# A fused layer-norm, expert and state-space kernel: softplus in one table set, diagonal states spread out, tiles of B taken from SBUF

## The chip, the cores and the metric

The kernel runs on one core of a Trainium2 chip. The metric is device time in microseconds (us) of one execution. The engines are PE (TensorE, matmul), DVE (VectorE), ACT (ScalarE), POOL (GpSimd) and SP (SyncE, which issues the plain DMAs). Each engine runs its own instructions in order and waits for the others by semaphores.

## The reference, cut to what matters

Four sequences of 512 tokens with 256 channels go through three parts: half an expert feed-forward, a selective state-space layer with 16 states, half the same feed-forward again. The change touches the middle part only:

```python
x_proj = x @ W_x.T
dt_x, Bm, Cm = jnp.split(x_proj, [R, R + N], axis=-1)      # R = 64, N = 16
dt = jax.nn.softplus(dt_x @ W_dt.T + b_dt)
dA = jnp.exp(jnp.einsum('bld,dn->bldn', dt, -jnp.exp(A_log)))
dBx = jnp.einsum('bld,bln,bld->bldn', dt, Bm, x)
h = dA_t * h + dBx_t                                        # scan over l
y_t = jnp.einsum('bdn,bn->bd', h, C_t)                      # plus x * D
```

## The kernel before, in words

A batch is one sequence. Channels lie on the partitions in two halves k = 0, 1, so one state of one batch is a tile of 128 x 1024 (two halves of 512 time steps). There are 64 states in all, s = 16 b + n, and each goes through a fixed line of engines:

- ACT: `decay(s)` writes da, two Exp of 128x511 (L663).
- dBx is made in one of two ways. In a *plain* state, dt x (tile `dtx_t`, time on the partitions) is multiplied by one column of B for each of four blocks of 128 time steps; ACT makes some of the four tiles (`outer`, L679, B read from `b_t` in SBUF) and DVE the others (`outer`, L1405, B read from `B_T`, which lies in the PSUM bank `Y`). `BY_DVE` says how many tiles DVE makes. PE then transposes the four tiles into a PSUM bank pair (`turn_dbx`, L1030). In a *diagonal* state (`DIAG`), PE multiplies `dtx_t` by a 256 KB block-diagonal matrix of B (L1037), which SP has loaded from memory (L384) into one of two buffers; no tile is made.
- DVE: the scan h = da h + dBx (L1421), da in SBUF and dBx in PSUM.
- POOL: the product gs = h C (L523), both operands in SBUF, C loaded by SP (L354).
- PE: `add(s)` transposes the product into the sum `YA` in PSUM (L1054). It also frees one of the two gs buffers for POOL.

The rings: four da and hs buffers (the scan of s waits for the product of s-4), two gs buffers (the product of s waits for `add(s-2)`), three plain tiles.

While batch b is scanned, batch b+1 is prepared: `project` (PE, L983), `project_copy` (ACT, L630), `project_bt` (PE transposes B into `B_T`, L994; DVE copies it into `b_t`, L1361), `project_z` (PE, L1003), softplus, `turn_dt` (PE, L1014) and `project_dtx` (DVE, L1390). Softplus is written as max(z,0) + ln(1+e) plus a rounding correction, with e = exp(-|z|). ACT does Abs, Relu (L637), Exp (L641), Identity (L650) and Ln (L657, a table set of its own); DVE does L1370 (for batch 0 the two lines L1373 and L1375), L1381 and L1384, each with one operand in a PSUM bank. All batches after the first use the one bank `T`, one half at a time.

At the turn from one batch to the next, DVE's `add_y` (L1457) adds `YA` to x after the last `add` of the batch, between the scans of n = 1 and n = 2, and takes the statistics of the result (L1177) after n = 2. POOL normalises tiles of 128x256 (L469) after the products of n = 5 to 8 (6 to 9 in batch 0) and eight such tiles before batch 0.

Before batch 0 there is a prologue: softplus(0), the last shared-expert gate `shared_gate(0, 3, 1)` (Tanh, L576), `turn_dt(0)`, the first tiles. In batch 3, ACT also does four Tanh pieces (L584).

Of the kernel before, what the change touches and what calls it, by code (L numbers as in the profile page):

```python
# [27 lines left out]
def macaron_kernel(nc, x, w_xT, w_dtT, b_dt, a_log, d_skip, router_w, gate_w, up_w, down_w,  # L28
# [23 lines left out]
    BY_DVE = ((2, 2, 2, 1, 1, 1) + (0,) * 6 + (1, 0, 1, 0),) + ((1, 1, 0, 1) + (0,) * 6 + (1, 0, 1, 0, 1, 0),) * 2 + ((0,) * 16,)  # L52
    DIAG = (tuple(range(6, 12)),) + (tuple(range(4, 10)),) * 2 + ((4, 7, 9, 13),)
# [6 lines left out]
    SHARED = E  # L60
    assert D == F == KC * P and L == 512 and GT == 16 and E == 8 and NR == 18 and N == 16
# [14 lines left out]
    with ExitStack() as ctx:  # L76
# [3 lines left out]
        def sem(name):  # L80
# [22 lines left out]
        neg_half = sb("neg_half", [P, LT])  # L103
        e_less = sb("e_less", [P, E])
# [123 lines left out]
        pj_all, pj_copy, pj_bt, pj_btc, pj_z, pj_abs, pj_max, pj_exp, pj_u, pj_w, pj_rest, pj_ln, pj_sum, pj_dt, pj_tp, pj_dtx = (  # L228
            sem(f"pj_{s}") for s in ("all", "copy", "bt", "btc", "z", "abs", "max", "exp", "u", "w", "rest", "ln", "sum", "dt", "tp",
# [191 lines left out]
        def _(pool):  # L421
# [8 lines left out]
            nc.gpsimd.memset(neg_half[:], -0.5)  # L430
            nc.gpsimd.memset(before[:], 1.0)
# [125 lines left out]
        def _(act):  # L557
# [85 lines left out]
            def project_u(b, k):  # L643

                if k == 0:
                    act.wait_ge(pj_exp, b + 1)
                    act.wait_ge(pj_max, KC * (b + 1))
                else:
                    act.wait_ge(pj_dt, KC * b + 1)
                nc.scalar.activation(pj_bank(b, k), w_exp[:, k], ACT.Identity, bias=1.0).then_inc(pj_u, 1)  # L650

            def project_ln(b):

                act.wait_ge(pj_exp, b + 1)
                if b > 0:
                    act.wait_ge(pj_sum, KC * b)
# [93 lines left out]
            nc.scalar.preload_act_table(ACT.Exp)  # L750
# [30 lines left out]
        def _(pe):  # L781
# [4 lines left out]
            def ln_transposes(c, q):  # L786
                pe.wait_ge(ln_xn, GT * c + 2 * q + 2)
                if c == 2:
# [197 lines left out]
            def project_bt(b):  # L986
# [4 lines left out]
                else:  # L991
                    pe.wait_ge(sc_dve, states_by("dve", N * (b - 1) + 4 + 3))
# [12 lines left out]
            def turn_dt(b, h):  # L1005

                pe.wait_ge(pj_dt, KC * (b + 1))
                if b > 0 and h > 0:
                    pe.wait_ge(pj_dtx, 2 * b + h)
                dst = YA[h] if b == 0 else T  # L1010
# [55 lines left out]
            def scan(b):  # L1066
                more = b + 1 < BATCH
                for n in range(N):
                    s = N * b + n
                    if more and n == 3:  # L1070
# [14 lines left out]
                    late = (2, 1, 0, 0)[b]  # L1085
# [4 lines left out]
                    if more and n - int(b == 0) in (8, 10):  # L1090
                        turn_dt(b + 1, (n - 8) // 2)
# [74 lines left out]
        def _(dve):  # L1166
# [384 lines left out]
```

## Time and profile before

| | us |
|---|---|
| median of 3 runs | 441.34 (440.18 to 441.75) |
| the profiled execution | 441.44 |
| its span, first to last instruction | 439.6 |
| first scan to last product of POOL | 142.8 to 330.1 |

Busy shares over the span are PE 92%, DVE 75%, ACT 63%, POOL 64%; the granted TensorE clock is 0.996. A share over the span mixes the expert parts, where PE is busy, with the scan, which takes some 187 us of the 440. A timeline row reads: start, duration of the merged run, engine, line, operation, output and inputs, count, and in brackets the idle time before it and what ended it. The duration of a single instruction overlaps the next one's by some 0.08 us on DVE, so the step from one start to the next is a little shorter.

### The profile page before, as it was taken

To read this page: it belongs to the slowest core of one execution; us is meant where nothing else is said; L and a number is where in the kernel's file an instruction comes from. 1 tells how busy PE (TensorE), PEld (TensorE's weight loads), DVE (VectorE), ACT (ScalarE), POOL (GpSimd) and SP (SyncE) were. 2 spreads that over 40 slices of the span, in tenths; PEclk is the share of its full clock that TensorE was granted. 3 is DMA by queue.
4 is the path that set the end of the run, shared out by engine and by line. 5 is a ranking of instruction groups with operands and counts; after the bars stand their busy time and mean duration, and the time that the engine had idled before them with its cause. 6 is when DMAs were issued, how large, how long until landed. Compare 5 with 4: busy or idle time off the path is not lost. (4 is left out here: it accounts for less than half of the span.)

```text
span 439.6 us, 8329 instructions
## 1 busy us (share of the span) xinstructions
PE 402.4 (92%) x2716; PEld 278.4 (63%) x2716; DVE 329.5 (75%) x518; ACT 275.0 (63%) x501; POOL 281.1 (64%) x216
## 2 busy tenths in 40 slices
PE   6899899999996899899989997989999899899995
PEld 5537444444454689777977797879994556344452
DVE  4678565553388988999999999989887775456552
ACT  1430465564248799897999899997962210556553
POOL 7204356643328589997999799988891006487553
PEclk9899999999999999999999999999999999999999
DMA  8958115842604226463536453443320534334311
GB/s 250 385 179 264 48 54 167 284 174 101 204 10 91 73 82 180 81 144 106 186 75 118 141 176 73 115 157 92 121 72 0 172 107 120 99 118 135 111 60 48
DMA packets 50808, 56.84 MB, mean 129 GB/s; under 512 B 16329, under 2 KB 35597, under 8 KB 50768
## 3 DMA queue, kind: packets, MB, share of 16 engines
q1 hardware_dynamic: 46624, 45.78, 35.0%
q0 software_dynamic: 4144, 10.54, 8.0%
q8 instruction: 23, 0.38, 0.4%
q14 instruction: 17, 0.14, 0.1%
HBM read 41.14 MB, written 16.48 MB: 131 GB/s over the span
## 5 line engine op out<-in xcount | busy, mean ns | idle before, releaser
L523 POOL TENSOR_TENSOR gs<-hs,c_sb 128x1024 f32<-128x1024 f32 x63 | 148.3, 2380 | 18.7 <-DVE hs L1421 11.4
L1421 DVE TENSOR_TENSOR_SCAN hs<-da,bank 128x1024 f32<-128x1024 f32 x64 | 144.1, 2273 | 4.1 <-PE bank L1030 2.1
L663 ACT ACTIVATE da<-dt_sb,a_neg 128x511 f32<-128x511 f32 x128 | 84.5, 713 | 2.4 <-DVE dt_sb L1384 1.2
L1054 PE MATMUL bank<-ident,gs 128*128 128x128 f32 x504 | 66.3, 275 | 7.5 <-POOL gs L523 5.9
L1054 PEld LDWEIGHTS bank<-ident,gs 128*128 128x128 f32 x504 | 55.9, 141 | 12.1 <-POOL gs L523 9.8
L679 ACT ACTIVATE dbx_t<-dtx_t,h_sb 128x256 f32<-128x256 f32 x145 | 62.1, 498 | 1.6 <-DVE dtx_t L1390 1.4
L879 PE MATMUL bank<-xnT,w_gu 128*128 128x512 f32 x112 | 50.8, 601 | 0.0
L1030 PE MATMUL bank<-ident,dbx_t 128*128 128x128 f32 x336 | 44.2, 274 | 6.8 <-DVE hs L1421 4.1
L477 POOL DMA_INDIRECT da<-rows,row_token x29 | 30.6, 1055 | 29.7 <-DVE row_token L1292 21.2
L1030 PEld LDWEIGHTS bank<-ident,dbx_t 128*128 128x128 f32 x336 | 37.5, 141 | 12.2 <-DVE hs L1421 5.9
L591 ACT ACTIVATE th<-bank,da 128x256 f32<-128x256 f32 x36 | 17.0, 473 | 43.1 <-PE bank L918 30.4
L918 PE MATMUL bank<-w_gu,tt 128*128 x72 | 35.6, 616 | 3.2 <-ACT tt L596 2.2
L498 POOL DMA_INDIRECT token_out<-y_sb,row_token x18 | 19.0, 1056 | 29.2 <-DVE y_sb L1338 26.3
L477 POOL DMA_INDIRECT da<-rows,row_half x14 | 14.7, 1054 | 35.5 <-DVE row_token L1297 27.2
L1328 DVE TENSOR_TENSOR h_sb<-th,bank 128x256 f32<-128x256 f32 x36 | 15.1, 420 | 28.0 <-ACT th L591 27.9
L915 PE MATMUL bank<-w_gu,tt 128*32 x72 | 34.3, 598 | 1.4 <-ACT tt L596 1.4
L879 PEld LDWEIGHTS bank<-xnT,w_gu 128*128 128x128 f32 x112 | 21.0, 194 | 22.4 <-issue 22.3
L915 PE MATMUL bank<-dtx_t,tt 128*32 128x512 f32 x72 | 34.3, 598 | 0.0
L574 ACT ACTIVATE hs<-bank 128x512 f32<-128x512 f32 x10 | 6.0, 597 | 40.0 <-PE bank L879 34.6
L596 ACT ACTIVATE tt<-bank 128x512 f32<-128x512 f32 (+1 forms) x40 | 22.1, 553 | 13.6 <-PE bank L933 12.3
L498 POOL DMA_INDIRECT out<-y_sb,row_token x18 | 19.8, 1098 | 16.1 <-DVE y_sb L1341 8.2
L562 ACT ACTIVATE xnT<-bank 128x512 f32<-128x512 f32 x24 | 13.9, 590 | 17.3 <-PE bank L807 17.2
(184 smaller groups left out, 787.1 us busy)
## 6 DMA issues: line engine op xcount, KB each, us to landing
c_sb<-c_dram SPq DMA_DIRECT2D x64, 256.0 KB, 3.3
rows<-xn_no SPq DMA_DIRECT2D x8, 516.0 KB, 5.4
diag_dram<-dbx_t SPq DMA_DIRECT2D x6, 512.0 KB
routing<-diag_dram SPq DMA_DIRECT2D x11, 256.0 KB, 2.8
slot_m<-diag_dram SPq DMA_DIRECT2D x11, 256.0 KB, 2.9
rows<-xn_no SPq DMA_DIRECT2D x1, 2064.0 KB, 9.4
x_sb<-in_x SPq DMA_DIRECT2D x4, 512.0 KB, 6.4
w_gu<-in_gate_w SPq DMA_DIRECT2D x2, 1024.0 KB, 10.2
```

What stands on the lines that cost most here:

```text
L477: nc.gpsimd.indirect_dma_start(out=xr[:, u, lo:hi], out_offset=None, in_=source, in_offset=bass.IndirectOffsetOnAxis(ap=row, axis=0), boun ...
L498: nc.gpsimd.indirect_dma_start(out=rows_back, out_offset=bass.IndirectOffsetOnAxis(ap=row_token[:, TILE[j]:TILE[j] + 1], axis=0), in_=y_sb ...
L523: nc.gpsimd.tensor_tensor(gs[:, s % 2], hs[:, s % RING], c_sb[:, s % RING].unsqueeze(1).to_broadcast([P, KC, L]), ALU.mult).then_inc(sc_g, 1)
L596: nc.scalar.activation(tt[:, (j + 1) % 2, lo:hi], T[:, lo * P:hi * P].rearrange("p (a t) -> p a t", t=P), ACT.Copy).then_inc(ff_tpc, 1)
L663: nc.scalar.activation(da[:, s % RING, k, 1:L], dt_sb[:, k, seq(s // N)][:, 1:L], ACT.Exp, scale=a_neg[:, k, s % N:s % N + 1]).then_inc(sc ...
L679: step = nc.scalar.activation(plain_buffer(s)[:, i, :], dtx_t[:, b % 2, i, :], ACT.Copy, scale=b_t[:, b, i, n:n + 1])
L879: last = nc.tensor.matmul(shared_banks(r, b, fo)[h], w_gu[:, k, SHARED, h * F + fo * P:h * F + (fo + 1) * P], xnT[:, k, b * L:(b + 1) * L] ...
L915: last = nc.tensor.matmul(H[j % 2][part, :], tt[:, j % 2, 2 + k, part], gu_part(i, g)[:, k, :] if g else w, start=(k == 0), stop=(k == KC ...
L918: last = nc.tensor.matmul(H[j % 2][:, :], tt[:, j % 2, 2 + k], w, start=(k == 0), stop=(k == KC - 1))
L1030: mm = nc.tensor.transpose(DBX[s % 2][:, k, i * P:(i + 1) * P], plain_buffer(s)[:, i, k * P:(k + 1) * P], ident[:])
L1054: mm = nc.tensor.matmul(YA[k][:, i * P:(i + 1) * P], products[:, k, i * P:(i + 1) * P], ident[:], start=(s % N == 0 and i == 0), stop=(s % ...
L1421: nc.vector.tensor_tensor_scan(hs[:, s % RING].rearrange(flat), da[:, s % RING].rearrange(flat), DBX[s % 2][:, :, :].rearrange(flat), 0.0, ...
```

## The change

- Softplus is rebuilt. ACT loads the set `natural_log_exp_and_others` by name, twice: before the first layer-norm copies, and again after `shared_gate(0, 3, 1)`. Relu goes; Identity becomes one instruction of 1024 that writes -(1+e) into SBUF (`neg_u`: half of `dtx_t` for batch 0, `y_sb` for the others). DVE then does `project_rest` (one of 1024, both inputs in SBUF), `project_max` (two of 512, one input in PSUM), `project_dt` (one of 1024, both inputs in SBUF) and `project_dtx` (one of 1024; two of 512 for batch 0).
- The two halves of z get a bank each (`T` and `Y`), so `B_T` in `Y` must have been copied away before the second half is written. `project_bt` on PE moves from n = 3 to n = 2, 1, 0 in batches 0, 1, 2, where it stands ahead of `turn_dbx(s+2)` and `add(s-1)`; DVE's copy moves from n = 4 to n = 3, 2, 1.
- DVE's `outer` reads B from `b_t` in SBUF, in all batches.
- In batches 1 and 2 the diagonal states are 4, 6, 8, 10, 12, 14 (before 4 to 9), and DVE makes one tile of each of the states 0 to 3 (before 0, 1, 3, 10, 12, 14).

```diff
-    BY_DVE = ((2, 2, 2, 1, 1, 1) + (0,) * 6 + (1, 0, 1, 0),) + ((1, 1, 0, 1) + (0,) * 6 + (1, 0, 1, 0, 1, 0),) * 2 + ((0,) * 16,)
-    DIAG = (tuple(range(6, 12)),) + (tuple(range(4, 10)),) * 2 + ((4, 7, 9, 13),)
+    BY_DVE = ((2, 2, 2, 1, 1, 1) + (0,) * 6 + (1, 0, 1, 0),) + ((1, 1, 1, 1) + (0,) * 12,) * 2 + ((0,) * 16,)
+    DIAG = (tuple(range(6, 12)),) + (tuple(range(4, 16, 2)),) * 2 + ((4, 7, 9, 13),)
...
+        def neg_u(b):
+            return dtx_t[:, 1].rearrange("p (k a) d -> p k (a d)", k=KC) if b == 0 else sg_h
...
-                nc.scalar.activation(dt_sb[:, k, seq(b)], pj_bank(b, k), ACT.Relu, bias=b_sb[:, k:k + 1]).then_inc(pj_max, 1)
...
-                nc.scalar.activation(pj_bank(b, k), w_exp[:, k], ACT.Identity, bias=1.0).then_inc(pj_u, 1)
+                nc.scalar.activation(neg_u(b), w_exp[:], ACT.Identity, bias=neg_one[:, 0:1], scale=-1.0).then_inc(pj_u, 1)
...
-            nc.scalar.preload_act_table(ACT.Exp)
+            nc.scalar.preload_act_table_set(EXP_LN)
...
             shared_gate(0, 3, 1)
+            nc.scalar.preload_act_table_set(EXP_LN)
...
-                    if more and n == 3:
+                    late = (2, 1, 0, 0)[b]
+                    if more and n == late:
                         project_bt(b + 1)
...
+            def project_rest(b):
+                dve.wait_ge(pj_u, b + 1)
+                nc.vector.scalar_tensor_tensor(out=neg_u(b), in0=neg_u(b), scalar=1.0, in1=w_exp[:],
+                                               op0=ALU.add, op1=ALU.add).then_inc(pj_rest, 1)
+            def project_max(b):
+                dve.wait_ge(pj_rest, b + 1)
+                for k in range(KC):
+                    nc.vector.scalar_tensor_tensor(out=neg_u(b)[:, k], in0=pj_bank(b, k), scalar=b_sb[:, k:k + 1], in1=neg_u(b)[:, k],
+                                                   op0=ALU.add, op1=ALU.max).then_inc(pj_max, 1)
...
-                nc.vector.tensor_tensor(pj_bank(b, k), log_w[:, k], pj_bank(b, k),
-                                        ALU.add if b == 0 else ALU.subtract).then_inc(pj_sum, 1)
-                dve.wait_ge(pj_sum, KC * b + k + 1)
-                nc.vector.tensor_tensor(dt_sb[:, k, seq(b)], pj_bank(b, k), dt_sb[:, k, seq(b)], ALU.add).then_inc(pj_dt, 1)
+                dve.wait_ge(pj_max, KC * (b + 1))
+                nc.vector.tensor_tensor(dt_sb[:, :, seq(b)], log_w, neg_u(b), ALU.add).then_inc(pj_dt, 1)
...
                 nc.vector.tensor_tensor(plain_buffer(s)[:, LT - mine:, :], dtx_t[:, b % 2, LT - mine:, :],
-                                        B_T[:, b, LT - mine:, n:n + 1].to_broadcast([P, mine, D]), ALU.mult).then_inc(sc_dve, 1)
+                                        b_t[:, b, LT - mine:, n:n + 1].to_broadcast([P, mine, D]), ALU.mult).then_inc(sc_dve, 1)
...
-                    if more and n == 4:
+                    if more and n == (3, 2, 1)[b]:
                         project_bt(b + 1)
...
+                    if more and n == 5 + late:
+                        project_rest(b + 1)
+                    if more and n == 6 + late:
+                        project_max(b + 1)
+                    if more and n == 7 + late:
+                        project_dt(b + 1)
+                    if more and n == 11 + late:
+                        project_dtx(b + 1)
```

## Rows read from the trace of the kernel before

**Rows 1.** Busy time by engine, the sum of 140 to 330 us:

```profile
sum 190.00, PE 176.61 PEld 158.46 DVE 179.97 ACT 170.83 POOL 170.45; mean PE 9.30 PEld 8.34 DVE 9.47 ACT 8.99 POOL 8.97
```

**Rows 2.** Timeline of POOL in the scan:

```profile
181.21 14.02 POOL L523 TENSOR_TENSOR gs<-hs,c_sb 128x1024 f32<-128x1024 f32 x6
...
271.84 23.53 POOL L523 TENSOR_TENSOR gs<-hs,c_sb 128x1024 f32<-128x1024 f32 x10
297.62 2.37 POOL L523 TENSOR_TENSOR gs<-hs,c_sb 128x1024 f32<-128x1024 f32 x1 [2.24 <-DVE hs L1421]
```

**Rows 3.** Timeline of DVE at the turn from batch 2 to 3:

```profile
289.39 1.28 DVE L1457 TENSOR_TENSOR x_sb<-x_sb,bank 128x512 f32<-128x512 f32 x2 [1.18 <-PE bank L1054]
290.59 2.28 DVE L1421 TENSOR_TENSOR_SCAN hs<-da,bank 128x1024 f32<-128x1024 f32 x1
```

**Rows 4.** Timeline of ACT in the prologue:

```profile
129.31 0.68 ACT L637 ACTIVATE dt_sb<-bank,b_sb 128x512 f32<-128x512 f32 x1
129.88 0.69 ACT L636 ACTIVATE w_exp<-bank,b_sb 128x512 f32<-128x512 f32 x1
...
131.02 1.07 ACT L641 ACTIVATE w_exp<-w_exp 128x1024 f32<-128x1024 f32 x1
132.11 1.28 ACT L657 ACT_TABLE_LOAD   x1
```

**Rows 5.** Timeline of DVE, last softplus step of the prologue and batch 0:

```profile
136.83 0.69 DVE L1384 TENSOR_TENSOR dt_sb<-bank,dt_sb 128x512 f32<-128x512 f32 x1
...
148.07 0.41 DVE L1405 TENSOR_TENSOR dbx_t<-dtx_t,bank 128x256 f32<-128x256 f32 x1
...
172.38 0.70 DVE L1370 SCALAR_TENSOR_TENSOR bank<-bank,w_exp 128x512 f32<-128x512 f32 x1 [0.74 <-ACT bank L650]
```

**Rows 6.** Timeline of PE, start of batch 0 and the turn to batch 2:

```profile
153.96 1.04 PE L1030 MATMUL bank<-ident,dbx_t 128*128 128x128 f32 x8
...
205.02 0.42 PE L994 MATMUL bank<-ident,th 16*128 16x16 f32 x4
...
208.13 1.95 PE L1037 MATMUL bank<-routing,dtx_t 128*128 128x128 f32 x16
...
240.52 1.88 PE L983 MATMUL bank<-xnT,w_x 128*96 128x512 f32 x4
242.24 1.04 PE L1030 MATMUL bank<-ident,dbx_t 128*128 128x128 f32 x8
243.11 1.04 PE L1054 MATMUL bank<-ident,gs 128*128 128x128 f32 x8
```

**Rows 7.** DMA issues: count, KB each, median us to landing:

```profile
routing<-diag_dram SPq DMA_DIRECT2D x11, 256.0 KB, 2.8
...
diag_dram<-h_sb SPq DMA_DIRECT2D x22, 2.0 KB, 3.7
```

**Rows 8.** Timeline of ACT at the start of batch 0:

```profile
154.16 0.59 ACT L630 ACTIVATE th<-bank 96x512 f32<-96x512 f32 x1 [2.26 <-PE bank L983]
```

**Rows 9.** Timeline of POOL at the start of batch 0:

```profile
145.15 4.87 POOL L523 TENSOR_TENSOR gs<-hs,c_sb 128x1024 f32<-128x1024 f32 x2 [4.12 <-DVE hs L1421]
...
163.29 2.38 POOL L523 TENSOR_TENSOR gs<-hs,c_sb 128x1024 f32<-128x1024 f32 x1 [0.41 <-PE bank L1054]
```

**Rows 10.** Single lines: count, duration min/median/max in ns, first and last start:

```profile
L1450 DVE TENSOR_TENSOR dbx_t<-hs,c_sb x2: 678/968/1259, 329.4 to 330.6; 128x512 f32<-128x512 f32 x2
L1405 DVE TENSOR_TENSOR dbx_t<-dtx_t,bank x20: 393/403/686, 139.7 to 274.1; 128x256 f32<-128x256 f32 x17, 128x512 f32<-128x512 f32 x3
L1357 DVE TENSOR_TENSOR x_sb<-xn_no,x_sb x3: 1217/1224/1225, 116.7 to 126.9; 128x1024 f32<-128x1024 f32 x3
L469 POOL TENSOR_SCALAR xn_no<-x_sb,mv,rstd x20: 1209/1221/1260, 131.4 to 270.7; 128x256 f32<-128x256 f32 x20
```

**Rows 11.** Timeline of all engines at the last product, POOL and DVE:

```profile
327.78 2.35 POOL L523 TENSOR_TENSOR gs<-hs,c_sb 128x1024 f32<-128x1024 f32 x1 [0.52 <-PE bank L1054]
...
329.42 1.86 DVE L1450 TENSOR_TENSOR dbx_t<-hs,c_sb 128x512 f32<-128x512 f32 x2
```

More of the change, by code:

```diff
@@ L227, in macaron_kernel @@
         a_ready = sem("a_ready")
-        pj_all, pj_copy, pj_bt, pj_btc, pj_z, pj_abs, pj_max, pj_exp, pj_u, pj_w, pj_rest, pj_ln, pj_sum, pj_dt, pj_tp, pj_dtx = (
-            sem(f"pj_{s}") for s in ("all", "copy", "bt", "btc", "z", "abs", "max", "exp", "u", "w", "rest", "ln", "sum", "dt", "tp",
+        pj_all, pj_copy, pj_bt, pj_btc, pj_z, pj_abs, pj_max, pj_exp, pj_u, pj_rest, pj_ln, pj_dt, pj_tp, pj_dtx = (
+            sem(f"pj_{s}") for s in ("all", "copy", "bt", "btc", "z", "abs", "max", "exp", "u", "rest", "ln", "dt", "tp",
                                      "dtx"))
@@ L701, in scan @@
                         project_exp(1)
-                        project_u(1, 0)
-                    if b < BATCH - 1 and n == 7 + int(b == 0):
-                        project_u(b + 1, 1)
+                    if b == 0 and n == 5:
+                        project_u(1)
                     if b == 0 and n == 6:
@@ L1005, in turn_dt @@
             def turn_dt(b, h):
[L1007 to L1010, printed above, removed]
+                pe.wait_ge(pj_dt, b + 1)
+                dst = pj_bank(b, h)
                 for i in range(2):
@@ L1089, in scan @@
                         skip(b, n - 5)
-                    if more and n - int(b == 0) in (8, 10):
-                        turn_dt(b + 1, (n - 8) // 2)
+                    if more and n - int(b == 0) in (8, 9):
+                        turn_dt(b + 1, n - int(b == 0) - 8)
                     turn = 12 if more else 9
@@ new lines, in project_dtx @@
+            def project_dtx(b):
+                halves = ((0, 1), (1, 2)) if b == 0 else ((0, 2),)
+                for lo, hi in halves:
+                    dve.wait_ge(pj_tp, 2 * b + hi)
+                    src = pair[3 if b == 0 else 1][:, lo:hi].rearrange("p h (i d) -> p (h i) d", d=D)
+                    nc.vector.tensor_tensor(dtx_t[:, b % 2, 2 * lo:2 * hi], src, xn[:, LT * b + 2 * lo:LT * b + 2 * hi, :],
+                                            ALU.mult).then_inc(pj_dtx, hi - lo)
@@ L1434, in scan @@
                         stats_of(2, b - 1)
[L1435 removed]
+                    late = int(b == 0)
+                    if more and n == (3, 2, 1)[b]:
                         project_bt(b + 1)
[L1437 to L1443 removed]
+                    if more and n == 5 + late:
[6 more added lines that the diff above has]
+                        project_dtx(b + 1)
             def last_product():
@@ L1492, in _ @@
             shared_hidden(0, 3, 0)
-            for k in range(KC):
-                project_w(0, k)
-            for k in range(KC):
-                project_dt(0, k)
-            for h in range(2):
-                project_dtx(0, h)
+            project_rest(0)
+            project_max(0)
+            project_dt(0)
+            project_dtx(0)
             outer(0)
```

63 lines of the change are left out of this document (21 added, 42 removed).

## The prediction

> **What bounds the kernel now.** I read the scan alone, since the change touches nothing else. First the busy time by engine over 140 to 330 us [rows 1]: VectorE is busy for 180 of 190 us, ScalarE for 171, GpSimd for 170. By that view VectorE is the bound, but a mean over four batches says nothing about which wait ends last. So next GpSimd's own timeline [rows 2]: 14.02 us for six products is 2.34 us each, 23.53 us for ten is 2.35, without a gap. The ten that begin at 271.84 are states 9 to 15 of batch 2 and 0 to 2 of batch 3. The reader is to see that inside a batch GpSimd always finds a finished scan. It idles only at a turn: 2.24 us before product 3 of batch 3. VectorE's timeline at that turn says why [rows 3]: product 15 ends at 271.84 + 7 x 2.353 = 288.31, TensorE adds it, `add_y` starts at 289.39 (an idle time ended by that add), the scan of n = 2 follows, then statistics and the scan of n = 3. The chain is thus GpSimd through a batch, then TensorE and VectorE through the turn. Time taken from ScalarE or VectorE in mid-batch buys nothing as long as GpSimd finds its scans ready; time put on GpSimd, or on the path to `add_y`, counts in full.
>
> **Softplus in one set.** In the prologue VectorE and ScalarE are the chain. Two Relus go at a step of 129.88 - 129.31 = 0.57 us [rows 4], so Exp ends 1.14 us earlier, at 130.95. The Identity of 1024 isn't shown; I take the Exp of that shape, 1.06, so it ends near 132.0, and Ln, without its load of 1.28 [rows 4], near 133.1. On VectorE, `project_rest` and `project_dt` have both inputs in SBUF at 1024, as the combine of 1.22 us [rows 10]; the two halves of `project_max` take 0.69 each at most [rows 5], 1.25 with overlap. 132.0 + 1.22 + 1.25 + 1.22 = 135.7 against 136.83 + 0.69 = 137.52 now [rows 5]: 1.8 us earlier, if nothing else stands in the way. On ScalarE the Tanh gate now takes a load before and a named load after it (133.1 + 1.28 + 0.6 + 1.28 = 136.3); that is hidden behind VectorE's `project_dtx` and first tile, and costs 0.6 at most if they come sooner.
>
> In batches 0 to 2, ScalarE loses two loads and two Relus and gains two tiles in batches 1 and 2; VectorE loses about 0.5 us of softplus (eight of some 0.69 against 3 x 1.22 + 2 x 0.69) and two tiles of 0.40 [rows 10]. The wait of 0.74 us at 172.38 [rows 5] may go too. All of that lies beside GpSimd's products: I count 0, with 4.5 us as the other end (1.4 of waits, 1.5 and 1.6 of work; a rival below). One load for the first Tanh of batch 3 is at most 1.28; I take 0, ScalarE being 19 us short of full [rows 1].
>
> **The diagonal states.** As many as before. A pair of a diagonal and a plain state costs TensorE, by steps (0.87 from 242.24 to 243.11 [rows 6], and 1.95 less the same 0.17 of overlap), 1.78 + 0.87 for dBx and 2 x 0.87 for the adds: 4.39 us against GpSimd's 4.69 for two products. So TensorE keeps up: 0, with 0.4 a pair as the bound where a turn of dt or xn falls in the pair. SP still issues six loads and six writes a batch, but loads at n = 9, 11, 13 now stand among the writes for the next batch and ahead of C loads. A load has at least two products, 4.7 us, before TensorE wants it; it lands in 2.8 and a write in 3.7 [rows 7]. I count 0; were they served strictly in turn, 3.7 + 2.8 - 4.7 = 1.8 us a time.
>
> **`project_bt` moved forward.** It waits for ScalarE's `project_copy`, and behind it on TensorE now stand `turn_dbx` and `add`. At the start of batch 0, `turn_dbx` of state 4 ran at 153.96 [rows 6], while the copy starts only at 154.16 and takes 0.59 [rows 8]. With 0.42 for the transposes of B [rows 6], `turn_dbx` starts at 155.17, 1.2 late, and so do `add(1)`, scan 4 and GpSimd's product 3, which needs that add. GpSimd's idle 0.41 at 163.29 [rows 9] swallows a part: 0.8. At the turn from batch 1 to 2, `project(3)` runs from 240.52 to 242.40, and `turn_dbx` and the last add followed at 242.24 and 243.11 [rows 6]. The copy (0.59) and the transposes (0.42) now come between: 243.4, again 1.2 late, all of it on `add_y`. In batch 1 the copy is old: nothing. Sum 2.0, bounds 0.8 and 2.4.
>
> **B from SBUF.** This decides. The one VectorE multiplication in the scan with both inputs in SBUF is the last product, L1450. Its two instructions took 1259 and 678 ns [rows 10]. The first started at 329.42, under a GpSimd product that ran from 327.78 to 330.13 [rows 11]; 329.42 + 1.26 = 330.68, which is GpSimd's end plus 0.55, about the work of 512 columns. The tiles of L1405, one input in PSUM, stayed at 393 to 403 ns (686 for the wide ones) in the same company [rows 10]. So I read: VectorE with two SBUF inputs doesn't run beside a GpSimd instruction that reads SBUF; it waits for its end. One event, but a sharp one. What GpSimd loses while VectorE runs, no row shows: between 0 and VectorE's whole duration. I take the whole, since two that can't run together in one order hardly can in the other.
>
> The Trainium skill says this outright ("SBUF — State Buffer", section "Who interferes with whom"): a VectorE instruction with two SBUF inputs and a GpSimd instruction that reads SBUF share a read interface, and the later one blocks for the whole of the earlier. The trace agrees with VectorE's half (1.26 against 0.68 us); that GpSimd blocks too, no run here shows. By the rule the sum is the one below; by the row alone it is the first rival.
>
> The change makes 4 `project_rest`, 4 `project_dt` and 16 tiles of that kind.
> - Prologue: rest, dt and the tiles of states 0, 1, 2 meet eight back-to-back normalisations of 1.22 us from 131.4 on [rows 10]. Each waits 0 to 1.22; five at the mean of 0.61 are 3.05. With the 1.8 gained: +1.25, bounds -1.8 and +4.3.
> - Start of batch 0: the tile of state 4 comes at 148.07 [rows 5], with products 0 and 1 running from 145.15 to 150.02 [rows 9]. It waits 1.95; scan 2, the last shared result, `add(0)` and `project(1)` are queued behind it: +2.0, bounds 0 and 2.35. Tiles 3 and 5 meet an idle GpSimd.
> - Inside the batches GpSimd stands still for six of 1.22 (rest and dt of batches 1 to 3) and eight tiles of 0.40 (states 12 and 14 of batch 0; 0, 1, 2 of batches 1 and 2): 7.3 + 3.2 = +10.5, bounds 0 and 10.5. States 3 of both batches fall where GpSimd waits anyway. VectorE's own waits, half a product or 1.17 each, fall into its lead over GpSimd: 0; the other end is 1.17 at the six and at four first tiles, +11.7.
>
> Sum: 1.25 + 2.0 + 0.8 + 1.2 + 10.5 = 15.75. The profiled execution took 441.44 us (span 439.6), the median 441.34, so they are one basis: 457 us.
>
> **Rivals.**
> - *Only VectorE waits; GpSimd loses nothing.* For it: the row shows no more. Against: sharing would then be one-sided. 441.4 + 1.25 + 2.0 + 2.0 = 446.7.
> - *VectorE is shut out.* Products follow each other every 2.34 us at 2.35 each [rows 2], so no gap may open until GpSimd runs out of scans. Then each of ten occasions (six large, four first tiles) costs GpSimd the instruction and a scan of 2.28 [rows 3]: 6 x 3.50 + 4 x 2.68 = 31.7, in all 441.4 + 1.25 + 4.0 + 31.7 = 478. Against: L1450 ran as soon as GpSimd ended, though nothing came after it there.
> - *Nothing excludes anything*, and the 1.26 us had another cause: -1.8 + 2.0, 441.6 us, no change.
> - *Faster: VectorE is the bound after all*, and nothing excludes. For it: 180 of 190 us [rows 1]. Against: no gap in GpSimd's runs. It decides if GpSimd finds a scan unfinished in mid-batch. Then 1.8 of the prologue, waits of 1.4 in batch 0, 0.5 a batch of softplus and four tiles of 0.40 come off, less 2.0 for `project_bt`: 441.4 - 1.8 - 1.4 - 1.5 - 1.6 + 2.0 = 437.1.
>
> **How the numbers follow.** The forecast gets 0.58 (its own range 449 to 464, from half of GpSimd's loss to a part of VectorE's waits), one-sided waiting 0.12, shut out 0.07, no change 0.13, faster 0.10. Slower is the first three less what spills, 0.76; same 0.13; faster 0.11. About 0.5%, 2.2 us, is what this kernel's measurement can tell from no change. The range 440 to 467 leaves out the faster case and the shut-out one.
>
> **What would show it.** Right: `project_rest`, `project_dt` and the tiles have long and scattered durations, ending a constant time after a GpSimd product; products beside them exceed 2.38 us or show gaps; GpSimd busy or blocked grows by some 10 us; `turn_dbx` of state 4 and the last add of batch 1 wait for L630; no table load is left in batches 0 to 2. Wrong: those VectorE instructions hold 1.22 and 0.40 us under a running product, or GpSimd's runs break in mid-batch for want of scans.

## The result, and the profile after

The changed kernel takes 458.85 to 463.95 us in three runs, 460.02 in the middle, against 440.81 us (440.18 to 441.75) for the kernel before. A fourth run, at 466.91, is over 1.5% above the fastest, counts as slow and is left out. The ratio is 1.0455, with a 95% interval of 1.0374 to 1.0535: slower by 4.6%, some 20 us. The forecast was 457.0, range 440 to 467.

The profiled execution took 458.85 us, its span 457.1, so 17.5 us more span than before. It is the shortest of the three; where the others lose up to 5 us more, no trace shows. The same instruction in both traces says where they came in: this is by how much later it starts after the change.

| from | to | later at the end by | gained in between |
|---|---|---|---|
| start of the kernel | first scan | 0.2 | 0.2 |
| first scan | add of state 0 | 2.0 | 1.8 |
| add of state 0 | POOL product 3 of batch 0 | 4.75 | 2.75 |
| there | POOL product 3 of batch 1 | 7.3 | 2.55 |
| there | POOL product 0 of batch 2 | 12.85 | 5.55 |
| there | POOL product 1 of batch 2 | 14.85 | 2.0 |
| there | POOL product 3 of batch 3 | 17.5 | 2.65 |

Nothing is lost behind that: the last product is 17.5 late too. POOL's timeline in the scan, whose rows of before are in [rows 2, 9]:

```profile
131.51 11.69 POOL L476 TENSOR_SCALAR xn_no<-x_sb,mv,rstd 128x256 f32<-128x256 f32 x8
145.34 4.87 POOL L530 TENSOR_TENSOR gs<-hs,c_sb 128x1024 f32<-128x1024 f32 x2 [2.15 <-DVE hs L1425]
154.59 2.34 POOL L530 TENSOR_TENSOR gs<-hs,c_sb 128x1024 f32<-128x1024 f32 x1 [4.38 <-PE bank L1059]
160.79 2.36 POOL L530 TENSOR_TENSOR gs<-hs,c_sb 128x1024 f32<-128x1024 f32 x1 [3.86 <-PE bank L1059]
...
178.12 2.19 POOL L476 TENSOR_SCALAR xn_no<-x_sb,mv,rstd 128x256 f32<-128x256 f32 x1
...
187.52 14.57 POOL L530 TENSOR_TENSOR gs<-hs,c_sb 128x1024 f32<-128x1024 f32 x6
...
216.07 5.68 POOL L530 TENSOR_TENSOR gs<-hs,c_sb 128x1024 f32<-128x1024 f32 x2
221.73 1.22 POOL L476 TENSOR_SCALAR xn_no<-x_sb,mv,rstd 128x256 f32<-128x256 f32 x1
...
225.26 2.21 POOL L476 TENSOR_SCALAR xn_no<-x_sb,mv,rstd 128x256 f32<-128x256 f32 x1
...
234.50 11.70 POOL L530 TENSOR_TENSOR gs<-hs,c_sb 128x1024 f32<-128x1024 f32 x5
248.75 4.98 POOL L530 TENSOR_TENSOR gs<-hs,c_sb 128x1024 f32<-128x1024 f32 x2 [2.56 <-DVE hs L1425]
...
259.17 2.37 POOL L530 TENSOR_TENSOR gs<-hs,c_sb 128x1024 f32<-128x1024 f32 x1 [2.37 <-PE bank L1059]
```

Two kinds of loss stand in it. First, instructions that became longer. A normalisation (L476) of 1.22 us takes 2.19 and 2.21; two products take 5.68 where an undisturbed pair takes 4.70; six take 14.57 against 14.02 in [rows 2]. Second, gaps: 4.38 and 3.86 at the start of batch 0, and in batch 1 one of 2.56 for want of a scan, in mid-batch, where before there was none. The two gaps at the start of batch 0 in the kernel before, 1.81 and 2.75 us shorter:

```profile
152.58 2.35 POOL L523 TENSOR_TENSOR gs<-hs,c_sb 128x1024 f32<-128x1024 f32 x1 [2.57 <-PE bank L1054]
156.04 2.36 POOL L523 TENSOR_TENSOR gs<-hs,c_sb 128x1024 f32<-128x1024 f32 x1 [1.11 <-PE bank L1054]
```

DVE's timeline names what stood against them:

```profile
148.27 2.21 DVE L1409 TENSOR_TENSOR dbx_t<-dtx_t,h_sb 128x256 f32<-128x256 f32 x1
...
176.71 2.51 DVE L1385 TENSOR_TENSOR dt_sb<-tt,y_sb 128x1024 f32<-128x1024 f32 x1
...
193.04 1.80 DVE L1409 TENSOR_TENSOR dbx_t<-dtx_t,h_sb 128x256 f32<-128x256 f32 x1
...
218.06 1.47 DVE L1371 SCALAR_TENSOR_TENSOR y_sb<-y_sb,w_exp 128x1024 f32<-128x1024 f32 x1 [1.46 <-ACT y_sb L658]
...
225.14 1.23 DVE L1385 TENSOR_TENSOR dt_sb<-tt,y_sb 128x1024 f32<-128x1024 f32 x1
...
241.15 5.33 DVE L1409 TENSOR_TENSOR dbx_t<-dtx_t,h_sb 128x256 f32<-128x256 f32 x1
```

Line these up with POOL's rows. The tile at 148.27 ends at 150.48, and POOL's pair of products at 145.34 + 4.87 = 150.21. The tile at 241.15 ends at 246.48, and POOL's run of five at 234.50 + 11.70 = 246.20. Both end 0.27 to 0.28 us after POOL, one after 2.21 us and one after 5.33; undisturbed, a tile takes 0.40. That is VectorE waiting for GpSimd. The row at 225.14 shows the other direction: `project_dt` starts first and takes an undisturbed 1.23, until 226.37; POOL's normalisation, started at 225.26, is the one that takes 2.21, 0.99 more. So between a VectorE instruction and a product, whichever comes second waits, and so does a normalisation that comes second. A normalisation that is already under way is another matter. POOL and DVE in the prologue:

```profile
134.98 1.22 POOL L476 TENSOR_SCALAR xn_no<-x_sb,mv,rstd 128x256 f32<-128x256 f32 x1
...
135.52 1.23 DVE L1385 TENSOR_TENSOR dt_sb<-tt,dtx_t 128x1024 f32<-128x1024 f32 x1
```

`project_dt` starts 0.54 us into that normalisation, and both take their undisturbed time. In e4, e5 and e7, below, the same instruction does so too (1.23 us each).

The third loss is on PE, in its timeline at the start of batch 0 and at the turn from batch 1 to 2, where before has [rows 6]:

```profile
153.32 1.09 PE L1059 MATMUL bank<-ident,gs 128*128 128x128 f32 x8 [3.68 <-DVE x_sb L1308]
154.25 3.37 PE L990 MATMUL bank<-xnT,w_x 128*96 128x512 f32 x4
158.30 0.42 PE L1001 MATMUL bank<-ident,th 16*128 16x16 f32 x4 [0.68 <-ACT th L637]
...
248.73 1.09 PE L1035 MATMUL bank<-ident,dbx_t 128*128 128x128 f32 x8 [3.08 <-DVE hs L1425]
...
251.24 1.97 PE L1035 MATMUL bank<-ident,dbx_t 128*128 128x128 f32 x8
...
256.68 0.42 PE L1001 MATMUL bank<-ident,th 16*128 16x16 f32 x4 [0.68 <-ACT th L637]
```

and the two stretches by themselves (the last columns are the granted clock, the DMA share and GB/s):

```profile
150.00:160.00 10.00, 6.00 (x28) 3.34 (x29) 6.24 (x7) 4.16 (x10) 2.55 (x2) 0.83 0.21 66
250.00:260.00 10.00, 9.24 (x50) 6.51 (x48) 7.18 (x7) 5.57 (x12) 6.79 (x4) 0.83 0.38 125
```

`project` takes 3.37 us where it took 1.88, and eight transposes take 1.97 instead of 1.09. In both stretches PE had just stood still, for 3.68 and 3.08 us, behind a late VectorE, and the granted clock is 0.83. With two levels, 2.4 and 1.2 GHz, 0.83 over 10 us means 3.4 us at the lower one.

### The profile page after: what moved, and what is told of

It reads as the page before. It is cut to its first block and busy times, and to the rows that moved or that the text cites. A ratio compares the mean times of both kernels' runs of the same rounds, so it can differ in the third digit from the quotient of the medians.

```text
span 457.1 us, 8294 instructions
## 1 busy us (share of the span) xinstructions
PE 406.7 (89%) x2716; PEld 279.2 (61%) x2716; DVE 340.2 (74%) x501; ACT 267.8 (59%) x490; POOL 289.3 (63%) x217
## 5 line engine op out<-in xcount | busy, mean ns | idle before, releaser
L530 POOL TENSOR_TENSOR gs<-hs,c_sb 128x1024 f32<-128x1024 f32 x63 | 150.7, 2412 | 27.5 <-PE bank L1059 14.3
L1059 PEld LDWEIGHTS bank<-ident,gs 128*128 128x128 f32 x504 | 57.0, 142 | 11.8 <-POOL gs L530 7.9
L687 ACT ACTIVATE dbx_t<-dtx_t,h_sb 128x256 f32<-128x256 f32 x149 | 63.6, 496 | 0.8 <-DVE dtx_t L1393 0.8
L1035 PE MATMUL bank<-ident,dbx_t 128*128 128x128 f32 x336 | 45.3, 279 | 11.0 <-DVE hs L1425 7.6
L886 PE MATMUL bank<-xnT,w_gu 128*128 128x512 f32 x112 | 51.9, 612 | 0.0
L476 POOL TENSOR_SCALAR xn_no<-x_sb,mv,rstd 128x256 f32<-128x256 f32 x20 | 29.5, 1479 | 0.0
```

Source lines behind the costliest of these rows:

```text
L476: nc.gpsimd.tensor_scalar(xn[:, i], x_sb[:, i, :], mv[:, i, 0:1], rstd[:, i:i + 1], ALU.subtract, ALU.mult).then_inc(ln_xn, 1)
L530: nc.gpsimd.tensor_tensor(gs[:, s % 2], hs[:, s % RING], c_sb[:, s % RING].unsqueeze(1).to_broadcast([P, KC, L]), ALU.mult).then_inc(sc_g, 1)
L687: step = nc.scalar.activation(plain_buffer(s)[:, i, :], dtx_t[:, b % 2, i, :], ACT.Copy, scale=b_t[:, b, i, n:n + 1])
L886: last = nc.tensor.matmul(shared_banks(r, b, fo)[h], w_gu[:, k, SHARED, h * F + fo * P:h * F + (fo + 1) * P], xnT[:, k, b * L:(b + 1) * L] ...
L1035: mm = nc.tensor.transpose(DBX[s % 2][:, k, i * P:(i + 1) * P], plain_buffer(s)[:, i, k * P:(k + 1) * P], ident[:])
L1059: mm = nc.tensor.matmul(YA[k][:, i * P:(i + 1) * P], products[:, k, i * P:(i + 1) * P], ident[:], start=(s % N == 0 and i == 0), stop=(s % ...
```

## Experiments

Each is a variant of one of the two kernels. Ratios are to the kernel before, run on the same chip.

**B from SBUF alone** (e1): before, and only VectorE's tiles read B from SBUF.

```diff
+                    dve.wait_ge(pj_btc, b + 1)
...
-                                        B_T[:, b, LT - mine:, n:n + 1].to_broadcast([P, mine, D]), ALU.mult).then_inc(sc_dve, 1)
+                                        b_t[:, b, LT - mine:, n:n + 1].to_broadcast([P, mine, D]), ALU.mult).then_inc(sc_dve, 1)
```

> The kernel before, with one thing changed: VectorE's tiles read B from SBUF instead of PSUM. Theory (VectorE with two SBUF inputs and GpSimd exclude each other, and GpSimd is the path): the tile of state 4 in batch 0 waits 2 us for a product, some 13 tiles inside the batches stop GpSimd for 0.4 us each, and one or two tiles may be shut out for more than one product as the tile of 5.33 us in the changed kernel was; 448 to 453 us. Rival (the tiles are cheap, and softplus or the moved transposes made the loss): within 1.5 us of 441.

Measured: 453.36 us, ratio 1.029 (1.0261 to 1.0319). One operand moved from PSUM to SBUF costs 12 us. DVE's timeline, then POOL's at the same place:

```profile
181.42 4.61 DVE L1406 TENSOR_TENSOR dbx_t<-dtx_t,h_sb 128x256 f32<-128x256 f32 x1
...
193.62 1.03 DVE L1406 TENSOR_TENSOR dbx_t<-dtx_t,h_sb 128x256 f32<-128x256 f32 x1
```

```profile
181.05 4.70 POOL L523 TENSOR_TENSOR gs<-hs,c_sb 128x1024 f32<-128x1024 f32 x2
188.31 2.37 POOL L523 TENSOR_TENSOR gs<-hs,c_sb 128x1024 f32<-128x1024 f32 x1 [2.56 <-DVE hs L1422]
```

The tile comes under the first of two products, lets a boundary between them pass, and ends at 186.03, 0.28 us after the second. By then VectorE is a scan behind, and GpSimd waits 2.56 us for it. The shut-out of the changed kernel thus occurs without its other parts. The six runs spread from 449.29 to 456.85 us, the profiled one being the shortest, and those of the kernel before from 440.44 to 442.71. That runs differ in which tiles are shut out would explain it, but no trace shows it.

**The schedule alone** (e2): before, with the new `DIAG` and `BY_DVE` of batches 1 and 2, B still read from PSUM.

```diff
-    BY_DVE = ((2, 2, 2, 1, 1, 1) + (0,) * 6 + (1, 0, 1, 0),) + ((1, 1, 0, 1) + (0,) * 6 + (1, 0, 1, 0, 1, 0),) * 2 + ((0,) * 16,)
-    DIAG = (tuple(range(6, 12)),) + (tuple(range(4, 10)),) * 2 + ((4, 7, 9, 13),)
+    BY_DVE = ((2, 2, 2, 1, 1, 1) + (0,) * 6 + (1, 0, 1, 0),) + ((1, 1, 1, 1) + (0,) * 12,) * 2 + ((0,) * 16,)
+    DIAG = (tuple(range(6, 12)),) + (tuple(range(4, 16, 2)),) * 2 + ((4, 7, 9, 13),)
```

> The kernel before with the new order of diagonal states and of VectorE's tiles in batches 1 and 2, B still read from PSUM. Theory: the schedule by itself is free, TensorE keeps up with GpSimd and the loads land in time; 441 us, 1.5 either way. Rival (diagonal states at the end of a batch crowd TensorE or the DMA queue): 444 or more, with GpSimd idle in mid-batch for TensorE's adds.

Measured: 444.32 us, ratio 1.0064 (1.0046 to 1.0081). Not nothing: 3 us. POOL's run through batch 1, unbroken before from 208.75 to the turn, has holes:

```profile
223.38 2.37 POOL L523 TENSOR_TENSOR gs<-hs,c_sb 128x1024 f32<-128x1024 f32 x1 [0.40 <-DVE hs L1421]
...
232.13 4.69 POOL L523 TENSOR_TENSOR gs<-hs,c_sb 128x1024 f32<-128x1024 f32 x2 [0.52 <-PE bank L1054]
237.09 9.60 POOL L523 TENSOR_TENSOR gs<-hs,c_sb 128x1024 f32<-128x1024 f32 x4 [0.26 <-PE bank L1054]
```

One hole waits for a scan and two for an add. Of the 4.0 us that the profiled run's span is longer, 1.2 lie before the first product, where nothing was changed, and 1.8 in batch 1. TensorE's rows, from one `turn_dbx` to that of the next pair of a diagonal and a plain state:

```profile
232.23 1.04 PE L1030 MATMUL bank<-ident,dbx_t 128*128 128x128 f32 x8
...
237.19 1.04 PE L1030 MATMUL bank<-ident,dbx_t 128*128 128x128 f32 x8
```

With the transposes of one normalised tile in it, the pair takes TensorE 4.96 us, more than GpSimd's two products. The scan was late for another reason. The old softplus goes back and forth between VectorE and ScalarE, and ScalarE now has more tiles to make in between: the view of waits puts 5.5 us, in four pieces, on VectorE's L1370 waiting for ScalarE's Identity (L650), where before it is under 0.8.

**One table set alone** (e3): before, with the two loads by name and nothing else.

```diff
-            nc.scalar.preload_act_table(ACT.Exp)
+            nc.scalar.preload_act_table_set("natural_log_exp_and_others")
...
             shared_gate(0, 3, 1)
+            nc.scalar.preload_act_table_set("natural_log_exp_and_others")
```

> The kernel before with Exp and Ln in one table set, nothing else. It takes six table loads, 7.7 us, off ScalarE in the scan. Theory (GpSimd is the path): 441 us, 1 us either way. Rival (ScalarE or VectorE is the path, since VectorE waits 1.4 us for ScalarE in batch 0): 438 or less.

Measured: 442.22 us, ratio 1.0014 (0.9994 to 1.0033). The loads were off the path.

**No tiles on VectorE** (e4): after, with ScalarE making all tiles from state 3 of batch 0 on.

```diff
-    BY_DVE = ((2, 2, 2, 1, 1, 1) + (0,) * 6 + (1, 0, 1, 0),) + ((1, 1, 1, 1) + (0,) * 12,) * 2 + ((0,) * 16,)
+    BY_DVE = ((2, 2, 2) + (0,) * 13,) + ((0,) * 16,) * 3
```

> The changed kernel, ScalarE making all tiles from state 3 of batch 0 on. Theory: the waits of 2.0 and 4.9 us of two tiles, GpSimd's idle time behind them, TensorE's half clock that follows both, and 0.4 us for each other tile under a product go: 449 to 453 us. What stays is softplus with two SBUF inputs and the moved transposes. Rival (softplus and the transposes make nearly all of the loss): 457 or more. Other rival (ScalarE becomes the path with 13 more tiles of 0.4 us): also 457 or more, with VectorE or TensorE waiting for ScalarE's tiles.

Measured: 454.79 us, ratio 1.03 (1.0281 to 1.0319), between the two. The tiles' losses are gone (the gap of 4.38 at 154.59 is 2.08 here, and eight products run unbroken up to the turn), but at the turn from batch 1 to 2 a new one has come. PE, then POOL:

```profile
249.69 0.42 PE L1001 MATMUL bank<-ident,th 16*128 16x16 f32 x4 [2.18 <-ACT th L637]
250.04 1.89 PE L1035 MATMUL bank<-ident,dbx_t 128*128 128x128 f32 x8
251.72 1.92 PE L1059 MATMUL bank<-ident,gs 128*128 128x128 f32 x8
```

```profile
253.81 2.37 POOL L530 TENSOR_TENSOR gs<-hs,c_sb 128x1024 f32<-128x1024 f32 x1 [4.53 <-PE bank L1059]
```

`project_bt` stands ahead of `turn_dbx` and `add` and waits for ScalarE's copy; the copy is now behind ScalarE's additional tiles, so PE stands still for 2.18 us and then works at the lower clock (1.89 for 1.09).

**`project_bt` behind the add** (e5): after, with these two lines moved.

```diff
-                    if more and n == late:
-                        project_bt(b + 1)
                     if s + 2 < STATES:
                         turn_dbx(s + 2)
...
+                    if more and n == late:
+                        project_bt(b + 1)
                     if more and n in (late, late + 1):
                         project_z(b + 1, n - late)
```

> The changed kernel with the transposes of B moved behind `turn_dbx` and `add` of the same step, ahead of the first half of z; nothing else. Theory (TensorE's wait for ScalarE's copy is 1.2 us at the start of batch 0 and 1.2 at the turn from 1 to 2): 2 to 2.5 us below the changed kernel's 462, so 459.5. Rival (the waits are hidden or only move): within 1 us of 462.

Measured: 455.79 us, ratio 1.0335 (1.0283 to 1.0386). By the ratios it is worth about 5 us, where 2 to 2.5 were expected; the two intervals leave room for 1 to 9.5. In its profiled run POOL goes through the end of batch 1 unbroken, and what is left at the start of batch 0 is the tile's wait, with the lower clock behind it (0.83 from 150 to 160 us here too):

```profile
155.32 2.35 POOL L530 TENSOR_TENSOR gs<-hs,c_sb 128x1024 f32<-128x1024 f32 x1 [5.26 <-PE bank L1059]
159.46 2.36 POOL L530 TENSOR_TENSOR gs<-hs,c_sb 128x1024 f32<-128x1024 f32 x1 [1.79 <-PE bank L1059]
...
233.53 19.38 POOL L530 TENSOR_TENSOR gs<-hs,c_sb 128x1024 f32<-128x1024 f32 x8
```

The 5.33 us of the tile at 241.15 did not come back, though the tile is still made. Whether a tile is shut out depends on when it comes.

**Both** (e7): e4 and e5 together.

> The run without tiles on VectorE (454.8 us), with the transposes of B moved behind as well. There GpSimd idled 4.5 us at the turn from batch 1 to 2, TensorE having waited 2.2 us for ScalarE's copy and then run at half clock. Theory: that goes, with 1.2 us at the start of batch 0: 449 to 451 us. Rival (ScalarE, which makes all tiles, is the path there and the copy is late anyway): 453 or more.

Measured: 447.06 us, ratio 1.0131 (1.0096 to 1.0166), a little better than the theory. `project_rest` still takes 1.28 to 3.25 us.

**Softplus without two SBUF inputs** (e6): e7, and the maximum is taken in place in PSUM, so that `project_dt` has one input there. It leaves out `project_rest` and ScalarE's Identity, that is, the rounding correction of softplus.

```diff
-                dve.wait_ge(pj_rest, b + 1)
...
-                    nc.vector.scalar_tensor_tensor(out=neg_u(b)[:, k], in0=pj_bank(b, k), scalar=b_sb[:, k:k + 1], in1=neg_u(b)[:, k],
-                                                   op0=ALU.add, op1=ALU.max).then_inc(pj_max, 1)
+                    nc.vector.tensor_scalar(pj_bank(b, k), pj_bank(b, k), b_sb[:, k:k + 1], 0.0, ALU.add, ALU.max).then_inc(pj_max, 1)
...
-                nc.vector.tensor_tensor(dt_sb[:, :, seq(b)], log_w, neg_u(b), ALU.add).then_inc(pj_dt, 1)
+                nc.vector.tensor_tensor(dt_sb[:, :, seq(b)], log_w, pair[3 if b == 0 else 1][:], ALU.add).then_inc(pj_dt, 1)
```

> As the run with no tiles and the transposes behind, and softplus without two inputs in SBUF: the maximum stays in PSUM, the last sum takes it from there, and the rounding correction (`project_rest` and ScalarE's Identity) is left out. So no VectorE instruction in batches 0 to 2 excludes GpSimd. Theory: three times 2 to 2.4 us of GpSimd go against that run; 443 to 445 us, what is left over 441 being the new order of states, which cost 3 us by itself. Rival (exclusion matters only for tiles, and the loss that is left comes from the schedule or the two banks of z): within 1.5 us of that run.

Measured: 441.78 us, ratio 1.0008 (0.9983 to 1.0032). The time is that of before, better than the 443 to 445 expected, and GpSimd is unbroken again:

```profile
224.98 21.13 POOL L530 TENSOR_TENSOR gs<-hs,c_sb 128x1024 f32<-128x1024 f32 x9
```

**Is GpSimd alone the path?** (e8): e3, and GpSimd's eight normalisations of batches 0 and 1 go to ScalarE, which had 7.7 us of table loads less. GpSimd loses 9.8 us of work.

```diff
-                    if b == BATCH - 1 and n == 3:
+                    if b > 0 and n == 3:
                         shift(b - 1)
-                    if 0 < b < BATCH - 1 and 5 <= n < 5 + LT:
-                        normalise(2, b - 1, (n - 5,))
...
-                    if not more and 6 <= n < 6 + LT:
+                    if b > 0 and 6 <= n < 6 + LT:
                         normalise(b - 1, n - 6)
```

> The kernel before with one table set and with the eight normalisations of batches 0 and 1 (1.22 us each) taken from GpSimd and given to ScalarE, as batch 2 has it already. Theory (GpSimd is the path inside a batch): up to 4.9 us a batch come off until VectorE, busy 97% of batch 1, is the path: 434 to 438 us. Rival (VectorE or TensorE binds as tightly as GpSimd): 440 to 442.

Measured: 441.75 us, ratio 1.0009 (0.9985 to 1.0032). Nothing is won, and the theory falls. The busy time of 200 to 290 us (PE, its weight loads, DVE, ACT, POOL), and a row of POOL's timeline:

```profile
200.00:290.00 90.00, 83.76 (x688) 76.30 (x689) 87.44 (x79) 84.15 (x163) 78.42 (x40) 1.00 0.48 127
...
226.78 4.90 POOL L525 TENSOR_TENSOR gs<-hs,c_sb 128x1024 f32<-128x1024 f32 x2 [0.40 <-DVE hs L1422]
```

GpSimd's busy time has fallen to 78.42 of 90 us, and it now waits for scans in mid-batch: VectorE, at 87.44 (87.23 in the kernel before), is as tight as GpSimd was.

**VectorE relieved too** (e9): e8, and VectorE's tiles of states 10, 12 and 14 of batches 1 and 2 go to ScalarE.

> The kernel before with one table set, GpSimd's eight normalisations of batches 0 and 1 given to ScalarE, and besides VectorE's six tiles of states 10, 12 and 14 of batches 1 and 2 given to ScalarE: VectorE is relieved of 6 x 0.40 = 2.4 us, GpSimd of its eight instructions of 1.22 = 9.8 us. Theory (GpSimd and VectorE are bound together in mid-batch, so that time is won only where both are relieved): 438 to 440 us, 1.5 to 2.4 below before, and the gaps of 0.40 us on GpSimd that wait for a scan become fewer. Rival (ScalarE, busy for 93% of mid-batch with the normalisations, becomes the third that is full): 441 us or more, with VectorE's or GpSimd's waits ended by ScalarE's decay or tile.

Measured: 444.6 us, ratio 1.0035 (1.0012 to 1.0058). The time is the rival's. In the profiled run, at 447.67 us the longest of twelve, ScalarE worked without a break from 217.4 to 251.1 us, and GpSimd, which was to win, waited 0.98, 0.75 and 1.42 us for adds on the way into batch 2. That ScalarE made those adds late is shown for the last alone: TensorE had waited 0.77 us for its copy. A tile costs VectorE 0.40 us and ScalarE as much (four in 1.70), so the move only shifts the load.

**Room on all three** (e11 and e10, both from e6, both without the rounding correction): e11 gives the eight normalisations to ScalarE, by the diff of e8; e10 instead puts `DIAG` of batches 1 and 2 back to the block 4 to 9.

> The changed kernel without any two-SBUF instruction of VectorE in batches 0 to 2 (ScalarE makes the tiles, the maximum is taken in place in PSUM, so that the rounding correction is left out), and besides GpSimd's eight normalisations of batches 0 and 1 given to ScalarE. Without the last step GpSimd ran unbroken, VectorE was busy for 82.0 of the 90 us from 200 to 290 and ScalarE for 78.3, so here, unlike in the kernel before, both others have room for GpSimd's 9.8 us. Theory (bound together: time is won where no engine of the three is full): 435 to 439 us. Rival (the turns, where GpSimd waits for TensorE and VectorE, give back what mid-batch wins, or ScalarE, with 4 x 0.59 us more in each of two batches, fills up): 440.5 us or more.

> The same kernel without the shift of the normalisations, but with the six diagonal states of batches 1 and 2 in a block (4 to 9), as before the change; the rounding correction is left out here too. Theory (the 3 us that the new schedule cost by itself came from VectorE and ScalarE, both nearly full in the kernel before, and this kernel has room on both): 441 to 443 us, no difference that can be told from the 441.8 with alternating states. Rival (alternating is dearer by its own order of work on TensorE and the loads): 438 to 440 us.

Measured: e11 437.37 us, ratio 0.9874 (0.985 to 0.9899); e10 440.73, ratio 0.9963 (0.9949 to 0.9977). e11 is the one version faster by more than 1%. Its busy times are level:

```profile
200.00:290.00 90.00, 85.50 (x711) 79.05 (x710) 85.50 (x68) 85.86 (x168) 79.96 (x41) 1.00 0.54 133
```

The same eight normalisations that were worth nothing in e8 are worth 1.3% of the time where VectorE and ScalarE have room. e10's time falls between its two ranges, but the kernel before took 442.6 us in this set of runs. By ratio, against e6 (in another set), the block order is 0.45% faster, 0.2 to 0.7% by the intervals, some 2 us. That is nearer the rival: much of e2's 3 us stays even with room on VectorE.

**A version that computes everything** (e12): e11 with the block order, and the correction back, each step with one input in PSUM.

```diff
+                both = pair[3 if b == 0 else 1][:]
-                nc.vector.scalar_tensor_tensor(out=neg_u(b), in0=neg_u(b), scalar=1.0, in1=w_exp[:],
+                nc.vector.scalar_tensor_tensor(out=both, in0=neg_u(b), scalar=1.0, in1=both,
                                                op0=ALU.add, op1=ALU.add).then_inc(pj_rest, 1)
+                dve.wait_ge(pj_rest, 2 * b + 1)
+                nc.vector.tensor_tensor(both, w_exp[:], both, ALU.add).then_inc(pj_rest, 1)
```

> A version that computes everything: GpSimd's eight normalisations and all tiles of VectorE given to ScalarE, the six diagonal states in a block again, project_bt behind the add, and the rounding correction back, but each of its VectorE instructions with one input in PSUM (maximum in place, then plus one minus u, then plus w, then plus the logarithm: 4 x 1024 elements wide or 2 x 512 a batch). Against the version without the correction (437.4, and about 2 less by the block order) VectorE has 2 x 1.22 us more a batch and ScalarE one of 1.04; VectorE was busy for 85.5 of 90 us there. Theory (no engine is full, and no VectorE instruction shuts GpSimd out): 435 to 439 us with the kernel before at 441 to 442.6. Rival (the three are bound together, and the 3.5 us a batch on VectorE and ScalarE fill both again): 440 to 443, no better than before.

Measured: 444.66 us, ratio 1.008 (1.0053 to 1.0108). Slower even than the rival: the correction costs all that e11 won and more. DVE's groups by line in the scan (busy us and mean ns), and POOL's gaps after them:

```profile
L1376 DVE TENSOR_TENSOR bank<-w_exp,bank 128x1024 f32<-128x1024 f32 x3 | 3.7, 1229 | 0.1
...
L1388 DVE TENSOR_TENSOR dt_sb<-tt,bank 128x1024 f32<-128x1024 f32 x3 | 3.6, 1194 | 0.0
```

```profile
215.75 2.37 POOL L532 TENSOR_TENSOR gs<-hs,c_sb 128x1024 f32<-128x1024 f32 x1 [1.31 <-DVE hs L1428]
219.06 9.45 POOL L532 TENSOR_TENSOR gs<-hs,c_sb 128x1024 f32<-128x1024 f32 x4 [0.94 <-DVE hs L1428]
```

Two things are seen here. Instructions of 1024 with one input in PSUM take 1.19 to 1.23 us on the mean beside GpSimd's products, and the products beside them 2.34 to 2.37: there is no exclusion, though they do what `project_rest` and `project_dt` do. And the 2.4 us more on VectorE a batch are nearly the 2.25 us that GpSimd waits for scans at that place, where e11 has no gap. Waits of 0.91, 1.10 and 2.16 us for adds follow in the same batch; they are not explained here.

## Why the prediction was right, point by point

**B and softplus from SBUF: right, in both halves.** The prediction took VectorE's wait from one row (L1450, [rows 10, 11]) and assumed that GpSimd pays as well. Both are now shown against products: tiles of 0.40 us end 0.27 to 0.28 us behind one, and products beside `project_rest` are late as well (5.68 us for a pair of 4.70). Normalisations of 1.22 that come second take 2.19 to 2.21. e1 and e12 show that the SBUF inputs are the cause and not the shape or the company: e1 moves one operand of the tiles, and `project_dt` with one input in PSUM takes 1.19 us, with two in SBUF up to 2.51. The Trainium skill's rule ("SBUF — State Buffer", section "Who interferes with whom") holds by that for products, whichever comes first. That `project_dt` takes 1.23 us inside a normalisation under way is not what it says, and that the wait can go on through several GpSimd instructions is more than it says.

**Inside the batches: +10.5 forecast, 10.75 measured** (2.55 + 5.55 + 2.65), but made up otherwise. The six large instructions cost GpSimd 0.85 to 0.99 us each, 5.7 in all, not 7.3, since VectorE has done part of its work when GpSimd arrives. The tiles in batch 0 cost 0.7. In their place stands one shut-out in batch 1: 2.56 us of GpSimd without a scan, and about 1 us behind it. That is the mechanism of the rival "VectorE is shut out", priced at 0.40 + 2.28 = 2.68, on one occasion of ten. The rest lies at the turns. "VectorE's own waits fall into its lead: 0" held for all the others. So the sum came out by luck: one term was too high, and a rival's mechanism made up for it.

**Start of batch 0.** The tile of state 4: +2.0 forecast, 1.8 measured (2.21 - 0.40). `project_bt`: +0.8 forecast, 2.75 measured. The wait for the copy and the transposes came as forecast: 0.68 + 0.42, 1.2 with the issue. The other 1.5 is `project` at half the clock (3.37 against 1.88), after PE had stood still behind VectorE's late tile. No term stood for that. e5 bears it out: without these transposes, but with the tile's wait, product 3 is still 3.42 us late (159.46 against 156.04), where it was 4.75.

**Turn from batch 1 to 2: +1.2 forecast, 2.0 measured**, the difference again at the lower clock (0.83 from 250 to 260). e5 moves `project_bt` back and wins some 5 us, but that is no price of these two terms: the shut-out was absent in its profiled run too, and the lower clock at the start of batch 0 stayed.

**Prologue: +1.25 forecast, 0.2 measured.** Both parts of this term were wrong. The 3.05 us of waits did not come: VectorE's `project_rest` is hardly delayed, 1.27 us, once ScalarE's Identity has ended, and `project_dt` runs inside a normalisation. It was GpSimd that waited; its eight normalisations took 11.69 us. The 1.8 us of gain did not come either. DVE, then PE, of this timeline:

```profile
132.70 1.27 DVE L1371 SCALAR_TENSOR_TENSOR dtx_t<-dtx_t,w_exp 128x1024 f32<-128x1024 f32 x1 [1.82 <-ACT dtx_t L658]
...
138.18 1.29 DVE L1393 TENSOR_TENSOR dtx_t<-bank,xn_no 128x512 f32<-128x512 f32 x2 [1.43 <-PE bank L1019]
```

```profile
135.04 0.66 PE L814 MATMUL bank<-ident,xn_no 128*128 128x128 f32 x4 [1.39 <-POOL xn_no L476]
...
137.54 1.04 PE L1019 MATMUL bank<-ident,dt_sb 128*128 128x128 f32 x8
```

and the same transposes on PE before:

```profile
133.86 0.66 PE L807 MATMUL bank<-ident,xn_no 128*128 128x128 f32 x4 [0.34 <-POOL xn_no L469]
```

`project_dt` ended at 135.52 + 1.23 = 136.75, 0.77 us earlier than before, though not at the 135.7 that was reckoned. But `project_rest` had held up a normalisation, TensorE transposes its result 1.18 us later than before, and `turn_dt`, queued behind that and 18 other matmuls, starts at 137.54 as it did before (137.57). So the delay of GpSimd is on the path here, and the gain is lost in it. Two wide tiles, 1.57 us for 1.28, make the 0.2.

**Table set and ACT's work: 0, right** (e3). **Schedule: 0, wrong** by 3 us in e2. The step that failed is "TensorE keeps up: 0". The pair of 4.39 us on TensorE leaves 0.3 under GpSimd's 4.69, and the 0.4 that was named as the bound for a pair with a turn of dt or xn came in: 4.96 us in e2. The wait for a scan there is ScalarE's and VectorE's. How the 3 us divide between the two is not shown.

**"The chain is GpSimd through a batch": half right.** Work put on GpSimd counts, and work taken from ScalarE buys nothing (e3), as was said. But work taken from GpSimd buys nothing either (e8). The ratios by steps tell what the parts are worth in this order: 1.0455 after; 1.0335 with `project_bt` behind the add; 1.0131 without the tiles; 1.0008 without rest and dt from SBUF. So 1.2%, 2.0% and 1.2% of the time, 5, 9 and 5 us, the first only to within 4. In the other order (e4 first) tiles and `project_bt` are 1.55% and 1.7%, which would follow if they share the shut-out and the clock.

**The sum, +15.75 for 17.5 in the trace, is closer than its parts.** The mechanism that decides, VectorE against GpSimd's products, was right both ways. But 1.05 us too much in the prologue and 1.6 in the six large instructions were made up for by the shut-out and by TensorE's lower clock, for which the sum had no term. That part is luck.

What stays open is why one tile gets in at the first end of a product (193.04, 1.80 us) and another is passed over at two (241.15) or one (e1, 181.42).

## What to carry to other kernels

Moving an operand from PSUM to SBUF can cost far more than its instruction: a VectorE instruction with both inputs in SBUF and a GpSimd product of two SBUF tiles serialise here, so before such a move, look for what GpSimd runs at that time. When a pipeline of several engines is balanced, the engine without gaps is not the only bound: relieve one by an experiment before calling it the path, since here 9.8 us off GpSimd were worth nothing in e8 and 1.3% in e11. A wait put ahead of TensorE's work costs its own length, and more if TensorE comes back at the lower clock.

## What was not expected of the hardware

- A VectorE tile of 0.40 us was held for 5.33 us, past two ends of GpSimd products, until GpSimd ran out of scans; in e1 for 4.61 us.
- A VectorE instruction with two SBUF inputs that started 0.54 us into a GpSimd normalisation took its 1.23 us and did not lengthen it (1.22); under a product, the same instruction waited for the end (2.51).
- In three places TensorE had stood still for 3.68, 3.08 and 2.18 us (the last in e4), and instructions soon after ran at about half speed (3.37 us for 1.88; 1.97 and 1.89 for 1.09), with a granted clock of 0.83 over the 10 us around the first two.
